# Two-layer cross-attention, experts and recurrent cell on one core: 23 products of two resident weights put ahead of TensorE's early work, and 90 empty instructions taken out later

## What is computed

```python
x = x + _L0_xattn_ref(_layernorm(x), ctx, ctx, ...)   # 16 heads of 8, with biases and an output projection
x = x + _L0_ffn_ref(_layernorm(x), ...)               # 8 experts, the two best of a gate, weighted by the gate
x = x + _L1_xattn_ref(_layernorm(x), ctx, ctx, ...)   # 16 heads of 8, no biases
x = x + _L1_ffn_ref(_layernorm(x), ...)               # gated cell over 128 steps, then tanh(x wo + c uo + bo)
```

## Time and profile before

| | |
|---|---|
| median of 3 runs | 842.12 us (841.3 to 842.35) |
| the profiled execution | 841.05 us |
| its span, first to last instruction | 839.2 us |
| TensorE busy, share of the span | 98% |
| mean granted TensorE clock | 0.992 of full |

### The profile page before, as it was taken

The page is one execution under the profiler, slowest core; times in us unless marked ns, Lnnn a source line. Parts: engine busy times, 40 slices in busy tenths (PEclk is TensorE's granted clock), DMA queues, the critical chain, the costliest instruction groups (busy, mean ns, idle before and its releaser), DMA issues.

```text
span 839.2 us, 42592 instructions
## 1 busy us (share of the span) xinstructions
PE 820.6 (98%) x15268; PEld 743.5 (89%) x15268; DVE 775.3 (92%) x2778; ACT 775.4 (92%) x2490; POOL 682.5 (81%) x1292
## 2 busy tenths in 40 slices
PE   8899999999999999999999999999999999999996
PEld 5688999999999999999999999999999999998884
DVE  6789999999999999999999999999999999999855
ACT  5899999999999999999999999999999999998874
POOL 5888998888888888888888888888888888887644
PEclk7999999999999999999999999999999999999999
DMA  9400000000000000000000000000000000000005
GB/s 345 175 3 3 2 4 4 4 3 4 3 3 4 4 4 3 4 3 4 3 4 4 4 4 4 3 3 4 3 4 3 4 3 4 4 4 3 3 3 201
DMA packets 6969, 17.74 MB, mean 21 GB/s; under 512 B 752, under 2 KB 2288, under 8 KB 6768
## 3 DMA queue, kind: packets, MB, share of 16 engines
q1 hardware_dynamic: 6336, 14.36, 4.5%
q10 hardware_dynamic: 432, 0.68, 0.3%
HBM read 10.84 MB, written 4.19 MB: 18 GB/s over the span
## 4 chain that ended last, share of the span: by engine, by line
PE 90%; DVE 4%; ACT 3%; issue 2%; POOL 1%; DVEq 0%; POOLq 0%; ACTq 0%
PE ps L458 15%; PE ps L480 13%; PE ps L393 13%; PE ps L378 8%; PE ps L423 7%; PE ps L554 6%; PE ps L540 5%; PE ps L329 4%; PE ps L358 4%; PE ps L437 3%; PE ps L343 3%; PE ps L320 2%; PE ps L404 2%; PE ps L321 2%; PE ps L493 1%
## 5 line engine op out<-in xcount | busy, mean ns | idle before, releaser
L1512 POOL TENSOR_TENSOR h<-Ex 128x512 f32<-128x512 f32 (+1 forms) x144 | 165.9, 1152 | 57.6 <-issue 51.2
L1106 DVE TENSOR_REDUCE mx<-ps 128x8 f32<-128x512 f32 (+1 forms) x288 | 167.0, 620 | 8.2 <-PE ps L378 7.9
L1120 DVE TENSOR_TENSOR Ex<-ps,mx 128x512 f32<-128x512 f32 (+1 forms) x288 | 170.8, 617 | 0.1
L819 ACT ACTIVATE ET<-ps 128x512 f32<-128x512 f32 (+1 forms) x288 | 166.0, 584 | 3.2 <-PE ps L393 2.9
L808 ACT ACTIVATE Ex<-Ex 128x512 f32<-128x512 f32 (+1 forms) x288 | 165.1, 608 | 2.0 <-DVE Ex L1120 1.8
L393 PE MATMUL ps<-w,Ex 128*128 128x128 f32 x1024 | 158.8, 275 | 0.1
L1212 DVE SCALAR_TENSOR_TENSOR acc<-ps,we,acc 128x128 f32<-128x128 f32 x448 | 147.9, 330 | 1.3 <-issue 0.2
L458 PEld LDWEIGHTS ps<-xT,w 128*128 128x128 f32 x1024 | 124.2, 191 | 24.6 <-issue 24.6
L458 PE MATMUL ps<-xT,w 128*128 128x128 f32 x1024 | 144.9, 284 | 0.0
L857 ACT ACTIVATE hT<-ps,w 128x128 f32<-128x128 f32 x512 | 140.1, 398 | 3.1 <-PE ps L458 2.8
L480 PE MATMUL ps<-w,hT 128*128 128x128 f32 x1024 | 139.0, 279 | 0.0
(11 more groups left out here) (108 smaller groups left out, 1847.4 us busy)
## 6 DMA issues: line engine op xcount, KB each, us to landing
cx<-ctx_dram SPq DMA_DIRECT2D x7, 512.0 KB, 12.5
x<-x_dram SPq DMA_DIRECT2D x7, 512.0 KB, 13.1
out_dram<-x SPq DMA_DIRECT2D x14, 256.0 KB, 2.7
w<-weights_dram SPq DMA_DIRECT2D x2, 512.0 KB, 5.4
w<-weights_dram SPq DMA_DIRECT2D x1, 576.0 KB, 8.7
out_dram<-x SPq DMA_DIRECT2D x4, 128.0 KB, 2.6
w<-weights_dram ACTq DMA_DIRECT2D x1, 328.0 KB, 4.4
w<-weights_dram ACTq DMA_DIRECT2D x1, 256.0 KB, 3.1
```

Of the source, the lines that this page charges most:

```text
L819: e.activation(ET[:, j % 2, r, lo:hi, :, :], b[:, 256 * lo:256 * hi].rearrange("p (c w q) -> p c w q", c=hi - lo, w=2), ACT.Copy).then_inc ...
L1106: e.tensor_reduce(mx[:, j % 2, r, 4 * lo:4 * hi], b[:, 256 * lo:256 * hi].rearrange("p (j k) -> p j k", k=64), AX.X, ALU.max).then_inc(sig ...
L1120: e.tensor_tensor(Ex[:, j % 2, r, 256 * lo:256 * hi].rearrange("p (j k) -> p j k", k=64), b[:, 256 * lo:256 * hi].rearrange("p (j k) -> p ...
L1512: e.tensor_tensor(u, v[:, :, :, 0:32], v[:, :, :, 32:64], ALU.add).then_inc(sig("half1"), 1)
```

## The change

It puts products of the resident weights `WK` and `WK1` (128x128, float32) ahead of nine steps of TensorE's program: 4 ahead of the query of tile 0, 4 ahead of the turning of tile 1, 2, 2 and 1 ahead of the scores of tiles 0, 1 and 2, 3 and 2 ahead of the queries of tiles 1 and 2, 4 ahead of the turning of the third quarter of the exponentials of tile 0 ("e2"), and 1 ahead of the turning of its reciprocal sums. They write to the bank that the step behind them is about to overwrite. It also raises `EVEN` from 2 to 7, which takes 18 empty instructions from each of five tiles, 90 in all.

```diff
-EVEN = 2
+EVEN = 7
+BUSY = {("q", 0): 4, ("turnx", 1): 4, ("S", 0): 2, ("q", 1): 3, ("S", 1): 2, ("q", 2): 2, ("e2", 0): 4,
+        ("rt", 0): 1, ("S", 2): 1}
...
+            def keep_busy(b, name, j):
+
+                for _ in range(BUSY.get((name, j), 0)):
+                    e.matmul(b[:, 0:128], wkv[:, WK, :], wkv[:, WK1, :], start=True, stop=True, skip_group_check=True)
+
...
                 b = bank(i, "turnx")
+                keep_busy(b, "turnx", j)
...
                 b = bank(i, "q")
+                keep_busy(b, "q", j)
                 e.wait_ge(sig("xT"), j + 1)
...
                 b = [bank(i, f"S{r}") for r in range(4)]
+                keep_busy(b[0], "S", j)
                 e.wait_ge(sig("qT"), j + 1)
...
                 b = bank(i, f"e{r}")
+                keep_busy(b, f"e{r}", j)
                 e.wait_ge(sig(f"E{r}"), j + 1)
...
                 b = bank(i, "rt")
+                keep_busy(b, "rt", j)
                 e.wait_ge(sig("rd"), j + 1)
```

## The result

The changed kernel takes 843.68 us (median of 8 runs, 843.24 to 845.8), the kernel before beside it 841.89 us (8 runs, 841.3 to 842.35). The profiled execution takes 843.45 us, its span is 841.7 us, 2.5 us longer than before. The eight runs fall into two groups: five from 843.24 to 843.91 us with a mean clock of 0.997 or 0.998, and three from 845.11 to 845.8 with 0.993 to 0.996. A mean of 0.997 to 0.999 is what a kernel has whose clock never falls early: in every profile the clock also falls behind TensorE's last product, here at 837.64 us, 4.0 us before the end.

A forecast was written before the change was run, and what follows sets the result against it. TensorE's work bounds the long middle, and a ring of waits between engines bounds the beginning. Tile 2's scores 2.71 us late plus 0 for empty instructions gave 842.12 + 2.7 = 844.8 us, range 841.6 to 846.2.

The forecast's parts named there:

- What bounds the kernel: TensorE's work paces the long middle, so a shift from the first groups reaches the end one for one.
- The place of the products: Nine steps: products stand behind the late bank wait, so each delays by 0.22 us; tile 2 scores 2.71 us late.
- The price of a product: Each added 128x128 float32 product on TensorE costs 0.22 us at full clock, nothing but the pace charged.
- the ring: First groups: scores, maxima and subtractions, query, copies, scores in a cycle; 22 of 23 products on it, 4.84 us.
- The start: Group 2: the query's wait ends at 8.36 us as before; four products put it at 9.24.
- The clock stays up: First groups: full clock holds past 10.28 us, likely but not sure; rival fall there, 847.6 us, chance 0.06.
- The empty instructions: Five tiles: taking out the 90 costs nothing the rows can show, taken as 0, at most 0.25 us either way.
- Hidden in the gaps: Rival, first groups: products fill waits, only the clock's gain, at most about 0.5 us, is left: 841.6 us, chance 0.10.
- Part of the shift is made up: Rival, first groups: other engines have cleared work when scores come late: 842.1 to 843.7 us, chance 0.09.
- TensorE's own work is the bound of the slow stretch: Rival, 10.28 to 20.52 us: full clock halves TensorE's 9.22 us of work, 4.6 us less: 837.5 us, chance 0.08.
- The sum: Whole kernel: 2.7 us added to the 842.12 us median gives 844.8 us.
- the main case: Whole kernel: products delay the first groups at full clock; own range 843.7 to 845.9 us, chance 0.67.

The follow-up runs named there:

- before, once more: The kernel before, unchanged, profiled a second time: 841.56 us.
- empty instructions out: Against the kernel before, only the 90 empty instructions taken out, no product added: 841.97 us, ratio 1.0009.
- products only: Against the kernel before, only the 23 products added at the change's places, empty instructions kept: 844.47 us, ratio 1.0039.
- 23 ahead of the wait: Against the changed kernel, the same 23 products issued before the bank wait, into an unused bank: 840.57 us, ratio 0.999 to the kernel before.
- doubled: Against the changed kernel, every product count doubled, 46 in all: 848.76 us, ratio 1.0089 to the kernel before.
- last fifteen: The changed kernel without its first eight products, 15 left from the scores of tile 0 on: 844.67 us, ratio 1.0025 to the kernel before.
- twelve ahead: Products ahead of the waits, only twelve, at queries and scores of tiles 0 and 1: 840.43 us, ratio 0.9988 to the kernel before.
- nineteen ahead: The 23 products ahead of the waits, without the four ahead of the turning of tile 1: 840.06 us, ratio 0.9975 to the kernel before.
- the first eight: The changed kernel with only the products ahead of tile 0's query and tile 1's turning: 841.44 us, ratio 1.0 to the kernel before.
- without any empty instruction: Against the kernel before, `EVEN = 99`: 1116 empty instructions out, no product added: 842.28 us, ratio 1.0005.

## Why the prediction was right

**What bounds the kernel: right in the main.** The start of the scores of tile 2 sets the whole time to within 0.7 us. For every kernel whose profile has the full clock behind that point, the span less that start is nearly one number:

```
kernel                    span     scores of tile 2   difference
before                    839.2    21.33              817.9
before, once more         839.7    21.77              817.9
changed                   841.7    23.94              817.8
empty instructions out    840.2    21.90              818.3
products only             843.1    25.50              817.6
23 ahead of the wait      838.7    20.89              817.8
doubled                   847.0    29.28              817.7
last fifteen              843.2    25.59              817.6
twelve ahead              838.5    20.89              817.6
nineteen ahead            838.5    20.73              817.8
```

The starts spread over 8.55 us and the differences over 0.7. In the two profiles left out the clock is at half behind the scores of tile 2, and the difference is larger: 841.4 - 22.01 = 819.4 with the first eight, 841.0 - 20.76 = 820.2 without any empty instruction. But "neither made up nor lengthened" is not exact. The shift of 2.61 us of the changed kernel grows to 2.86 at the scores at 120.03 us (now 122.89). GpSimd's key products then show it melt: 2.86 us at 150.36 (now 153.22), 2.58 at 332.05 (334.63), 2.44 at 368.48 (370.92), 2.40 at 599.30 (601.70), and 2.4 at the end. From 150 to 370 us TensorE is busy for 220.00 of 220.00 us in both profiles. Why some 0.4 us is made up there was not tried.

**The place of the products: right, and it is the step that decides.** The products stand behind `xT`, `D2`, `qT` and `ET1` in the trace as in the order. The run with the same products ahead of the waits shows that it is the place that costs, not the products as such: 3.05 us at the scores of tile 2. That the bank written differs too was not tried by itself; the releasers in the trace speak for the place.

**The price of a product: too low.** I took 0.22 each and no more. The block of four ahead of the query takes 0.99 us (7.45 to 8.44), the three behind `D2` 0.77 (14.07 to 14.84), the pairs ahead of scores 0.62 each (10.29 to 10.91, 16.05 to 16.67), the single one 0.39 (23.55 to 23.94). The block that has no wait in front, ahead of the turning of tile 1, takes 0.89, four times 0.22. So a block ahead of a query costs about 0.11 more than its pace, and one ahead of the scores about 0.2 more. The eight blocks on the ring sum to 0.99 + 0.89 + 0.62 + 0.77 + 0.62 + 0.55 + 1.00 + 0.39 = 5.83 us instead of 4.84. The sentence "nothing but the pace is charged" was the wrong one. Of these 0.99 us, 0.18 come back elsewhere on the ring: the pair ahead of the scores, for one, starts 0.14 us after `xT` has ended (10.15 to 10.29), where I had put 0.20.

**The start: an error the other way.** I had the query's wait end at 8.36 us "as before". It ended at 7.45, since the clock rose at 4.79 us in this execution and at 6.86 in that of before. That is no work of the change: TensorE's program is the same up to there, and in the runs of the experiments the rise is at 5.12, 5.26, 5.78, 6.40, 6.79, 7.11 and 7.38 us. From the query's wait to the scores of tile 2 the ring took 23.94 - 7.45 = 16.49 us where I had 24.04 - 8.36 = 15.68. The lead of 0.91 us and the 0.81 more nearly cancel: that the start at 23.94 us agrees so well with 24.04 is luck.

**The clock stays up: right for five runs of eight.** I gave the fall a chance of 0.06, as a trait of the kernel. It is one of the execution: the clock stays up in most, and in three of the eight runs, at 845.1 to 845.8 us, the mean clock is lower. That the reason is a short fall in these very groups was not seen in a profile of the changed kernel itself, but in that of the products alone.

**The empty instructions: right** at no cost that can be measured, tried with twelve times the dose.

**The rivals.** "Hidden in the gaps" is false for the change and true for the products ahead of the waits. I put the clock's gain there at 0.5 us. From 21.33 to 20.89 and 20.73 it is 0.4 to 0.6 in the profiles, and up to 1.0 against the second profile of the kernel before (21.77). From the scores of tile 0 to those of tile 2 the ring takes 10.8 to 10.9 us in the three kernels with hidden products, and 11.6 and 11.9 in the two profiles of the kernel before. Between the medians of the kernel with nineteen products and its kernel before it is about 2 us (840.06 and 842.23). Most executions of the kernel before are later than the one I read; how much of the 2 us is the clock was not tried. "Part of the shift is made up", 842.1 to 843.7 us, has the median of 843.68 in its range. But what it says did not happen in the ring, where the scores of tile 2 are 2.61 us late, close to the forecast 2.71; the 0.4 us that are made up go between 150 and 370 us. "TensorE's own work is the bound of the slow stretch", 837.5 us, is false: with a full clock and hidden products no run came below 839.4. With it falls the price by the rule of the Trainium skill ("TensorE: Matmul & The Clock Gate", section "Terms"): half of the slow stretch would be 5.1 us by this estimate, and 0.25% or some 2 us is what the best version won in the medians. This case does not agree with it.

**The sum** of 2.7 us stands against 1.8 in the medians, and 2.5 in the profiled spans. The measured 843.68 us lies inside the range from 841.6 to 846.2, but at the lower edge of the main case's own range, 843.7 to 845.9, and just below the 843.8 that I had called the line to "slower". I had given "slower" 0.70 and "same" 0.22, so the time is less well forecast than the mechanism. 0.23 us of the miss is that the median of the kernel before was 842.12 in the runs that I had and 841.89 with the later ones.

For the rest the traces hold a likely cause, which no experiment tried. In the kernel before, an early query is of use only if the normalized input `xn` of tile 1 is there as early, since its turning comes before the scores. In the run with only the empty instructions out, the query's wait ended at 7.65 us, and the scores of tile 0 still came at 9.87, since the turning stood idle for 0.76 us:

```profile
8.86 0.48 PE L350 MATMUL ps<-w,xn 128*128 128x128 f32 x1 [0.76 <-ACT xn L792]
```

In the second profile of the kernel before, the turning waits 0.25 us for `xn` as well. In the run without any empty instruction it waits for nothing, at 8.31 us, and the scores of tile 0 come at 9.17. With the products the turning comes only at 9.56 or 10.42 us, when `xn` is there, and a lead of the query goes through: in the changed kernel and in the run with the products alone the query's waits end at 7.45 and 8.31 us and the scores of tile 0 start at 10.91 and 11.76. So in these profiles an early rise of the clock helps the changed kernel each time and the one before only where `xn` is early, and a late `xn` lengthens only the one before. The prediction had neither, since it read one execution.

## What to carry to other kernels

Work that is put in to fill a wait has to be issued ahead of the wait that ends last. Where a step waits first for its buffer and then for its operands, find out which of the two comes late: filler that writes to the step's own buffer stands behind the first one, and each piece of it is then a delay on the ring. And before paying for a faster clock, read what part of the ring lies on the engine whose clock it is; here halving the pace of TensorE for 10 us cost 0.4 to 1.0 us in the profiles, and no more than some 2 us in the medians.

## What the runs showed that I had not expected

- The moment at which TensorE's clock first rises differs between executions by 2.6 us (4.79 to 7.38 us from the start), with the same instructions before it, and moves the first groups with it.
- The clock falls while TensorE is far from idle. In the run with the products alone it was busy for 6.95 of 10.24 us ahead of the fall, and for 1.71 of the last 3.41; in that with the first eight for 8.91 of 13.66, and for 1.91 of the last 3.42. The longest idle time of TensorE in the first of these was 1.26 us.
- A shift of the whole pipeline is partly made up in a stretch in which TensorE is busy all the time: 2.86 us at 150 us, 2.44 at 370.
- How steady a kernel runs depends on this beginning: with nineteen or 23 products ahead of the waits all runs of a kernel lie within 1.1 us, with twelve within 2.1, with only the first eight, behind their waits, within 2.7.
